# Dense attention of a conv and attention hybrid on one Trainium2 core: the first head by halves of queries, GpSimd's edge splitting behind a wait, VectorE's edge work and last sums in another order

## The reference, cut to what matters

```python
h = _group_norm(x, gn_gamma, gn_beta)
qkv = jnp.einsum('oc,bchw->bohw', qkv_w, h) + qkv_b[None, :, None, None]
...
attn = jax.nn.softmax(jnp.einsum('bhdn,bhdm->bhnm', q, k) * scale, axis=-1)
out = jnp.einsum('bhnm,bhdm->bhdn', attn, v).reshape(B, C, H, W)
return x + jnp.einsum('oc,bchw->bohw', proj_w, out) + proj_b[None, :, None, None]
```

## Time and profile before

| what | us |
|---|---|
| median of 3 runs | 2507.49 |
| lowest, highest | 2506.93, 2756.47 |
| profiled execution | 2505.68 |
| its span | 2503.9 |
| mean granted TensorE clock | 0.838 of full |

### The profile page before, as it was taken

The page is one execution under the profiler, slowest core; times in us unless marked ns, Lnnn a source line. Parts: engine busy times, 40 slices in busy tenths (PEclk is TensorE's granted clock), DMA queues, the critical chain, the costliest instruction groups (busy, mean ns, idle before and its releaser), DMA issues. The chain is left out here.

```text
span 2503.9 us, 26613 instructions
## 1 busy us (share of the span) xinstructions
PE 1892.9 (76%) x8906; PEld 869.7 (35%) x8906; DVE 1573.4 (63%) x3594; ACT 1021.7 (41%) x1662; POOL 714.1 (29%) x693
## 2 busy tenths in 40 slices
PE   1595786689578657579975888878878888978596
PEld 1121321332132124456641222322322325854356
DVE  3477778777776866645745575665566555634567
ACT  0241233314123314535542667656656662124251
POOL 2300630260063023014442312322322331137720
PEclk7696887789688878879975999989988987769797
DMA  3300300210030000021002111101011000024100
GB/s 100 92 3 25 83 9 20 60 40 2 25 92 1 20 8 1 1 81 39 1 17 75 41 30 38 32 27 39 28 28 37 4 4 14 2 62 52 10 4 35
DMA packets 55407, 80.26 MB, mean 32 GB/s; under 512 B 17201, under 2 KB 28455, under 8 KB 55024
## 3 DMA queue, kind: packets, MB, share of 16 engines
q1 hardware_dynamic: 44758, 69.14, 9.3%
q10 hardware_dynamic: 6426, 7.99, 1.4%
q0 software_dynamic: 4096, 1.58, 1.3%
HBM read 50.13 MB, written 24.68 MB: 30 GB/s over the span
## 5 line engine op out<-in xcount | busy, mean ns | idle before, releaser
L2486 DVE TENSOR_REDUCE f_half_max<-f_ring 128x1 f32<-128x512 f32 x512 | 334.8, 684 | 273.0 <-PE f_ring L2152 270.9
L2369 ACT ACTIVATE f_probs<-f_ST 128x512 f32<-128x512 f32 x512 | 292.8, 597 | 210.8 <-PE f_ST L2179 206.7
L2152 PE MATMUL f_ring<-f_stacks 96*128 96x512 bf16 x512 | 212.1, 415 | 54.5 <-DVE f_half_max L2486 28.1
L772 DVE TENSOR_REDUCE att_half_max<-att_ring 128x1 f32<-128x512 f32 x256 | 161.2, 683 | 101.5 <-PE att_ring L659 96.6
L2179 PE MATMUL f_ST<-f_stacks 99*128 99x512 bf16 x512 | 204.0, 403 | 10.4 <-ACT f_probs L2369 10.3
L755 ACT ACTIVATE att_probs<-att_ST 128x1024 f32<-128x1024 f32 x128 | 129.3, 1023 | 156.1 <-PE att_ST L684 155.9
L2196 PE MATMUL f_O<-f_probs,f_v_ext 128*32 128x512 f32 x1024 | 153.3, 674 | 0.1
L3202 POOL DMA_INDIRECT ti_row<-features,slot_from x128 | 126.9, 992 | 57.4 <-issue 57.4
L2152 PEld LDWEIGHTS f_ring<-f_stacks 96*128 96x128 bf16 x512 | 50.4, 99 | 258.8 <-DVE f_half_max L2486 162.6
L659 PE MATMUL att_ring<-stacks 96*128 96x512 bf16 x256 | 103.7, 471 | 46.5 <-DMA stacks<-parts_dram 25.9
L684 PE MATMUL att_ST<-stacks 96*128 96x512 bf16 (+1 forms) x512 | 137.8, 398 | 0.0
(11 more groups left out here) (585 smaller groups left out, 3552.7 us busy)
## 6 DMA issues: line engine op xcount, KB each, us to landing
f_stacks<-f_parts SPq DMA_DIRECT2D x192, 64.0 KB, 2.2
parts_dram<-l_parts SPq DMA_DIRECT2D x8, 768.0 KB, 3.6
stacks<-parts_dram SPq DMA_DIRECT2D x24, 256.0 KB, 9.5
stacks<-parts_dram ACTq DMA_DIRECT2D x24, 256.0 KB, 10.5
f_parts<-f_parts SPq DMA_DIRECT2D x8, 768.0 KB, 3.4
es_raw<-L_ffn_edge_index SPq DMA_DIRECT2D x8, 512.0 KB, 4.2
bm_mix<-mix SPq DMA_DIRECT2D x8, 512.0 KB, 9.0
xn_cm<-x SPq DMA_DIRECT2D x1, 2048.0 KB
```

The lines of the kernel that those rows point to most:

```text
L772: nc.vector.tensor_reduce(half_max[:, h % 2, t, n:n + 1], ring[:, i % RING], AX.X, ALU.max, negate=True).then_inc(reduced, 1)
L2152: nc.tensor.matmul(ring[:, i % RING], f.stacks[0:STACK, 0, at, t * P:(t + 1) * P], f.stacks[0:STACK, 1, at, n * BANK:(n + 1) * BANK], star ...
L2369: nc.scalar.activation(f.probs[:, s % PROBS, n * BANK:(n + 1) * BANK], ST[:, i % HALVES], ACT.Exp).then_inc(probs_ready, 1)
L2486: nc.vector.tensor_reduce(f.half_max[:, h % 2, t, n:n + 1], ring[:, i % RING], AX.X, ALU.max, negate=True).then_inc(reduced, 1)
```

## The change

Three things. Head 0's steps are reordered: its eight steps each still have 1024 columns, but as two tiles of keys for one half of the queries; four steps do the first half of the queries, four the second. So only four tiles of maxima and one row item come ahead of step 0; tiles 4 to 17 are spread over steps 0 to 7 by `FIRST_TILES`, and the second half's rows follow at step 3. `parts` runs by half for head 0, and counts 0, 1 for head 0 and h + 1 for later heads. GpSimd's split waits for the second count of `parts_ready`. VectorE takes two pieces of edge work a step from step 18, and what is left comes behind the normalisation.

```diff
+FIRST_TILES = (6, 8, 9, 11, 13, 14, 16, 18)
...
-    steps = [(g * share + j, m) for g in range(groups) for m in range(NT) for j in range(share)]
+    assert share == 1 and NC2 == 2
+    by_halves = [(0, [(m, n), (m + 1, n)]) for n in range(NC2) for m in range(0, NT, 2)]
+    steps = by_halves + [(h, [(m, n) for n in range(NC2)]) for h in range(1, heads) for m in range(NT)]
...
+    half = NT // 2
...
-    schedule("first", tiles(0, in_group))
-    for h in range(share):
-        schedule_rows("first", h)
+    schedule("first", tiles(0, half))
+    schedule_rows("first", 0, 0, [0])
+    at = half
     for s in range(len(steps)):
-        r = s + in_group + AHEAD
-        schedule(s, tiles(in_group if s == 0 else r, r + 1))
-        if (s + 1) % NT == 0 and s + in_group < len(steps):
-            schedule_rows(s, (s + in_group) // NT)
+        until = FIRST_TILES[s] if s < NT else s + NT + AHEAD + 1
+        schedule(s, tiles(at, until))
+        at = until
+        if s == half - 1:
+            schedule_rows(s, 1, 0, [1])
+        elif (s + 1) % NT == 0 and s + in_group < len(steps):
+            h = (s + in_group) // NT
+            schedule_rows(s, h + 1, h, list(range(NC2)))
...
             def scores_transposed(s):
-                h, m = steps[s]
-                if m == 0:
+                h, pieces = steps[s]
+                if s < NT:
+                    pe.wait_ge(rows_off, s // half + 1)
+                elif s % NT == 0:
                     pe.wait_ge(rows_off, NC2 * (h + 1))
                 if s >= 2:
                     pe.wait_ge(probs_ready, s - 1)
-                for n in range(NC2):
+                for i, (m, n) in enumerate(pieces):
...
                 for s in range(v * visit, (v + 1) * visit):
-                    h, m = steps[s]
-                    for n in range(NC2):
+                    h, pieces = steps[s]
+                    for i, (m, n) in enumerate(pieces):
                         at = width * (NC2 * (h % share) + n)
                         last = nc.tensor.matmul(O[at:at + width, :], k.v_ext[:, m, h, :],
-                                                probs[:, s % probs_ring, n * BANK:(n + 1) * BANK], start=(m == 0),
+                                                probs[:, s % probs_ring, i * BANK:(i + 1) * BANK], start=(m == 0),
                                                 stop=(m == NT - 1), tile_position=(0, at))
...
-                    if t == NT - 1 and n == NC2 - 1:
-                        parts(h)
...
+                    if n == NC2 - 1 and (t == NT - 1 or (h == 0 and t == half - 1)):
+                        parts(h, slice(0 if h else t + 1 - half, t + 1))
...
                 if beside is not None and s >= EDGES_FROM:
-                    for _ in range(1 if s < in_group + AHEAD + EDGES_FROM - 2 else 2):
+                    for _ in range(1 if s < EDGES_FROM + 4 else 2):
                         next(edge_steps, None)
-            if beside is not None:
-                for _ in edge_steps:
-                    pass
             if share == 1:
                 carry_off(groups - 1)
...
                 nc.vector.tensor_tensor(chunk(o_cm, n), chunk(o_cm, n), chunk(den, n), ALU.mult).then_inc(normed, 1)
+            if beside is not None:
+                for _ in edge_steps:
+                    pass
...
             def _(pool):
+                pool.wait_ge(parts_ready, 2)
                 beside.split(pool, edges_loaded, edges_linked, edges_coded)
```

More of the change, by code:

```diff
@@ L600, in schedule, with schedule_rows @@
         items.extend(new)
[L602 to L605, removed]
+    def schedule_rows(step, part, h, ns):
+        rows_at[step] = [part]
+        rows_of[part] = list(range(len(items), len(items) + len(ns)))
+        items.extend(("r", h, n) for n in ns)
     def tiles(lo, hi):
         return [("s", h, t, n) for h, t in (divmod(r, NT) for r in range(lo, min(hi, heads * NT))) for n in range(NC2)]
-    schedule("first", tiles(0, in_group))
-    for h in range(share):
-        schedule_rows("first", h)
+    schedule("first", tiles(0, half))
+    schedule_rows("first", 0, 0, [0])
+    at = half
     for s in range(len(steps)):
-        r = s + in_group + AHEAD
-        schedule(s, tiles(in_group if s == 0 else r, r + 1))
-        if (s + 1) % NT == 0 and s + in_group < len(steps):
-            schedule_rows(s, (s + in_group) // NT)
+        until = FIRST_TILES[s] if s < NT else s + NT + AHEAD + 1
[6 more added lines that the diff above has]
+            schedule_rows(s, h + 1, h, list(range(NC2)))
     order = {"s": {}, "r": {}}
@@ L661, in scores, with shift_rows @@
                                  stop=True).then_inc(ring_ready, 1)
[L663 to L667, removed]
+            def shift_rows(part):
+                pe.wait_ge(parts_ready, part + 1)
+                for i in rows_of[part]:
+                    _, h, n = items[i]
                     bank_free(i)
@@ L680, in scores_transposed @@
                     pe.wait_ge(probs_ready, s - 1)
-                for n in range(NC2):
+                for i, (m, n) in enumerate(pieces):
                     for j in range(per):
                         rows = STACK + 3 if j == per - 1 else STACK
-                        last = nc.tensor.matmul(ST[:, s % 2, n * BANK:(n + 1) * BANK],
+                        last = nc.tensor.matmul(ST[:, s % 2, i * BANK:(i + 1) * BANK],
                                                 k.stacks[0:rows, 1, per * h + j, m * P:(m + 1) * P],
@@ L728, in _, with rows @@
         def _(act):
-            def rows(h):
-                for i in rows_of[h]:
-                    n = items[i][2]
+            def rows(part):
+                for i in rows_of[part]:
+                    _, h, n = items[i]
                     act.wait_ge(ring_ready, i + 1)
@@ L773, in maxima, with parts @@
                                             negate=True).then_inc(reduced, 1)
-                    if t == NT - 1 and n == NC2 - 1:
-                        parts(h)
[L777 to L781, removed]
+                    if n == NC2 - 1 and (t == NT - 1 or (h == 0 and t == half - 1)):
+                        parts(h, slice(0 if h else t + 1 - half, t + 1))
+            def parts(h, ts):
+                a, p_ = shift[:, h % 2, ts], shift_parts[:, h % 2, ts]
+                dve.wait_ge(reduced, NC2 * (NT * h + ts.stop))
+                link(nc.vector.tensor_tensor(a, half_max[:, h % 2, ts, 0], half_max[:, h % 2, ts, 1], ALU.min))
                 link(nc.vector.tensor_copy(p_[:, :, 0], a))
```

## The result

The changed kernel takes 2568.57 us (median of four runs, 2567.08 to 2574.37) against 2508.65 for the kernel before (2506.93 to 2509.81, and one run of 2756.47 that the ratio leaves out): ratio 1.0245, 95% interval 1.0224 to 1.0267. It is slower, by 60 us. The forecast was 2560, its range 2510 to 2573. The profiled execution has a span of 2565.8 us, at nearly the same mean clock (0.839 against 0.838).

A forecast was written before the change was run, and what follows sets the result against it. No engine is busy throughout (TensorE 76%, VectorE 63%). Profiled 2505.7 + 44.5 (first head) + 5.0 (edge work, last carry-off) + 3.4 (clock falls) = 2558.6, or 2560 us on the median's scale; range 2510 to 2573.

The forecast's parts named there:

- Opening: Start of each image's dense attention: first exponential 10.2 us after the first maximum, a lead of 7.5; second chain ends at 14.1.
- Visits: Head 0's groups of eight attention matmuls (L702) lose their pairing: 3.5 us each instead of 1.87, four an image.
- fourth visit's price: Head 0's last group of eight attention matmuls, at step 9: 1.6 us more an image.
- Steps 2 to 7: From the second shift chain's end to step 8's transposed scores: 31.6 us, putting step 8 at 45.7 from the first maximum.
- the lock: Head 1's shift chain on VectorE is held by GpSimd's split instructions, ending at 22.5 instead of 18.7: 3.8 us lost.
- The first rival: Head 1's chain arrives over a microsecond earlier and escapes GpSimd's split: 22 us less in all, 2538 us; chance 0.17.
- the fall of 1.8: TensorE idles while head 1's chain is held, its clock drops, and the next group of attention matmuls loses 1.8 us.
- Edge part: Image end: third carry-off 4.15 us later, last 1.25 later; 5.0 us in all plus 3.4 for clock falls.
- Visits at 1.87 (2513.5): Second rival: head 0's groups of eight attention matmuls stay paired at 1.87 us, total 2513.5 us; chance 0.08.
- the faster one (2482): Third rival: head 0's attention matmuls hide behind a never-idle VectorE, step 8 comes at 27 us, total 2482; chance 0.07.
- The fourth rival: Image end: the last carry-off starts as the matmuls end, 2.9 us gained instead of 1.25 lost; 2544 us; chance 0.10.

The follow-up runs named there:

- edges alone: Kernel before with only the change's edge work order (two pieces a step from step 18, remainder behind the normalisation): 2517.12 us, ratio 1.0039.
- halves alone: Changed kernel without GpSimd's wait and with the edge pacing and remainder loop of before: 2546.27 us, ratio 1.0150.
- halves and wait (old edges): Changed kernel with the edge pacing and remainder loop of the kernel before; halves and GpSimd's wait stay: 2547.22 us.
- halves and edges (no wait): Changed kernel without GpSimd's wait; halves and new edge order stay: 2565.49 us.
- pairs kept: Changed kernel with the two tiles of a head 0 step on the array's two column halves (head 0's output differs): 2537.23 us.
- parted pairs: Kernel before with each head 0 visit's eight matmuls reordered, four on the first half of queries, then four on the second: 2504.70 us, ratio 0.9986.
- split behind head 1's chain: Changed kernel with GpSimd's split let go by the third shift chain (head 1's) in place of the second: 2565.40 us.
- edge work early: Kernel before with edge work begun at step 8 in place of 14, one piece a step to step 25, then two: 2505.80 us, ratio 0.9990.
- three early pieces: Kernel before with GpSimd waiting ahead of its third split instruction, and two edge pieces moved to step 7, one to step 11: 2492.26 us, ratio 0.9943.
- wait inside the split: Kernel before with GpSimd waiting for head 0's chain ahead of the third of its eight split instructions: 2499.45 us, ratio 0.9966.
- GpSimd's wait alone: Kernel before with only GpSimd's wait, its split let go behind head 1's shift chain: 2507.69 us, ratio 1.0003.

## Why the prediction was right, and where not

The runs around the change, as in the table of the result:

| profiled execution | to step 8 | 8 to 14 | 14 to third carry-off | to last carry-off | to the end | rest | median |
|---|---|---|---|---|---|---|---|
| edges alone | 143.7 | 62.4 | 156.2 | 55.8 | 53.1 | 2043.0 | 2517.1 |
| halves alone | 177.0 | 69.2 | 139.0 | 62.5 | 53.1 | 2042.9 | 2546.3 |
| halves and wait (old edges) | 184.0 | 69.2 | 134.5 | 62.4 | 53.1 | 2042.2 | 2547.2 |
| halves and edges (no wait) | 177.9 | 69.1 | 156.2 | 54.1 | 53.1 | 2047.1 | 2565.5 |
| after | 185.4 | 69.2 | 152.9 | 54.1 | 53.1 | 2051.2 | 2568.6 |

**Opening: right.** The first exponential stands at 10.2 in all four images, the second chain ends at 14.1, and the split is let go there (14.2).

**Visits: right, and shown.** 3.65 where 3.5 was said; pairs kept brings 1.94 back, and 8 to 14 falls from 69.2 to 62.4, the fourth visit's price. The stated reason was a little off: "neighbours have the same half" is not what matters, since parted pairs cost nothing; what matters here is that all eight of a visit are on one half. The Trainium skill, TensorE: Matmul & The Clock Gate, Part 3 on packing, has narrow matmuls at different tile positions run together in the array; the 1.94 of a visit on both column halves, against 3.65 on one, agrees with that.

**Steps 2 to 7: the sum right by luck, of two errors.** The opening at half clock was missing, and the lock was taken too long; the two nearly cancel. Counted from the first maximum, in the four images:

| mark | forecast | measured |
|---|---|---|
| first visit | 18.0 | 19.45, 20.49, 17.95, 19.19 |
| head 1's chain arrives | 31.75 | 33.23, 36.34, 31.73, 32.97 |
| head 1's chain ends | 36.6 | 36.65, 37.34, 36.58, 36.59 |
| step 8 | 45.7 | 46.61, 47.34, 45.40, 46.05 |

The chain arrives up to 1.5 us late in two images, and 4.6 in the second, where the opening's half clock lasted into the first visit (5.71). But it ends within 0.1 of the forecast in the three images where it met the split, because the split's end releases it, whenever it came. The chain took 2.4, 0, 3.9 and 2.6 us longer than its free 1.0, or 8.9 us, where the forecast has 4 x 3.8 = 15.2. The Trainium skill, SBUF — State Buffer, Who interferes with whom, has the blocked engine wait for the holder's whole instruction; this chain agrees (129.93 and 2.18 is the end of GpSimd's 129.73 and 2.35, within 0.03).

**The first rival's price: wrong.** "3.8 and the fall of 1.8 go, 22 in all: 2538". Two runs take the lock off head 1's chain (the split behind it, and no wait), and both bring step 8 forward (8.3 and 7.5 us in sum), but the medians move by 3 us each, the second with runs 19 us apart. The lock's 3.8 went, as far as there was one, but the fall of the clock did not go with it: behind the clean chains of the split behind head 1 the third visit still took 4.43, 3.65, 5.48 and 4.93 us, against 5.41, 5.44, 4.27 and 4.91 in after. Without the wait, 3.3 of it are given back between 14 and the third carry-off (156.2 for 152.9); in that stretch an image took 39.0 us where the visit of step 15 was at half clock (2.8 to 3.6 us: all four images without the wait, two of four in after) and 37.4 where it was not (1.94). What decides whether the clock falls there was not isolated. So in this change moving the lock behind head 1's chain was worth some 3 us and not 22, and the wait was worth next to nothing with the old edges.

**Edge part: right in place, and in size within its own run.** The last carry-off follows directly on the matmuls, the visit behind the third waits 3.04, and the fall of the clock that was counted in half of the images is in two of four. From 14 to the last carry-off the edge part adds 11.6 us alone (212.0 less 200.4), 8.8 on halves and 10.1 on halves with the wait, against 8.4 forecast. That after shows only 6.6 there against the kernel before is that in two images the clock does not fall at step 15; with the old edges, too, two images go without that fall once the wait is there (134.5, against 139.0 without the wait).

**What stays open.** By the medians the edge part costs 21 us on halves with the wait and 19 without, and its stretch explains nine to ten. The remainder is seen in the rest: 2051.2 and 2047.1, against 2042.2 and 2042.9. The runs of after (2567.1 to 2574.4) and of the old edges (2545.9 to 2548.5) lie so far apart that the 21 us are no accident of one execution; where they fall is read from one profile each. Between these two the rest differs behind the last image, by 9.6 us, and there the granted clock stood at its lower level for 490.3 and 456.7 us. The order of the edge work does not do that by itself: with the edge part alone the rest is 2043.0, and with halves alone 2042.9. Over all profiles of this study the rest was 2043.0 to 2054.5 in the five kernels with the new edge order, 2042.1 to 2046.4 in the seven with the old, and 2047.7 and 2041.9 in the two with a third (edge work early, three early pieces). Why the clock falls more often behind after was not settled. The forecast had nothing for it: its 52.9 us stand beside 53.2 measured within the dense attention, and the rest's 8.8 come on top.

**The other rivals.** Visits at 1.87 (2513.5) and the faster one (2482) fall with the visits; and with pairs kept, no lock on head 1's chain and the old edges, the halves are still not ahead at step 8, so the faster rival is out for a second reason: between the maxima VectorE waited for visits and products (2.54, 1.86 and 4.72 us in the first image of that run). The fourth rival is half right: the last carry-off starts as the matmuls end, but the matmuls end later.

## What to carry to other kernels

Before a product is moved, ask which others share its time on the array: the halves' earlier first exponential cost a pairing in every visit of that head, 1.7 us each, and the lead was gone by step 8, even where the pairs were kept. A wait that keeps two engines apart at one place moves the slow one into the next place: lay all the short chains of the other engine out on one time line, and split the long work around them, as the wait inside the split did for 0.3%. Work laid into the idle time that the trace shows, two pieces into 3.0 us and one into 1.75, shortened the stretch behind the third carry-off by 11.7 us and cost nothing ahead of it, while one piece in every step from 8 on lost most of the same gain again.

## What the runs showed of the hardware that was not expected

Matmuls on the two column halves ran side by side although in the program four of one half stood ahead of the four of the other (eight in 1.95 us, starts in twos, 13 ns apart); eight on one half took 3.65. How far apart in the order they may stand was not tried.

An instruction of VectorE's shift chains (0.16 to 0.18 us when free) that met a tensor-tensor of GpSimd ended with it: in these fourteen profiles 51 began while one ran, and each ended 0.02 to 0.04 us behind it. So the time at which the chain came hardly mattered: arrivals at 31.73, 32.97 and 33.23 ended at 36.58, 36.59 and 36.65.

The same instructions of the rest took 2041.9 to 2054.5 us from kernel to kernel. Behind the last image they took 1634.3 us where the granted clock stood at its lower level for 461.2 us (GpSimd's wait alone), and 1649.7 where it did for 504.0 (split behind head 1's chain). A change of ten microseconds in one stage is thus seen in that stage's own stretch with less doubt than in the total.
